# Causal attention with the value products of two units in a row, local attention with 64-row mask products

## What is computed

```
scores = q k^T / sqrt(8), masked where key > query
out    = softmax(scores) v, then a projection
```

```
x = attn_layer(shift_tokens(x)) + x      # 6 times
x = ffn_layer(shift_tokens(x)) + x
sim  = 8 * q k^T, masked outside a band of 32 keys before the query
out  = softmax(sim) v
```

## Time and profile before

| | us |
|---|---|
| Median of 3 runs | 5096.87 (5092.64 to 5099.63) |
| Profiled execution, device time | 5098.97 |
| Its span | 5097.2 |
| TensorE matmul busy | 4661.2 (91%) |
| VectorE busy | 3758.7 (74%) |
| ScalarE busy | 2797.7 (55%) |
| GpSimd busy | 2121.7 (42%) |

### The profile page before, as it was taken

The page is one execution under the profiler, slowest core; times in us unless marked ns, Lnnn a source line. Parts: engine busy times, 40 slices in busy tenths (PEclk is TensorE's granted clock), DMA queues, the critical chain, the costliest instruction groups (busy, mean ns, idle before and its releaser), DMA issues. The chain is left out here.

```text
span 5097.2 us, 170071 instructions
## 1 busy us (share of the span) xinstructions
PE 4661.2 (91%) x75792; PEld 2846.5 (56%) x75792; DVE 3758.7 (74%) x4270; ACT 2797.7 (55%) x3791; POOL 2121.7 (42%) x1691
## 2 busy tenths in 40 slices
PE   7858997999689869999999999999999999999998
PEld 5623333444233336774767567665776567747674
DVE  5667883333688659885898588867897688868895
ACT  4527774223477736554556556555565556546564
POOL 4330000001100046663666366635665466536661
PEclk9979998999799989999999999999999999999999
DMA  0021111000111121111111111111111111111110
GB/s 23 12 69 33 42 44 36 1 0 22 58 44 38 32 61 44 37 39 43 40 40 40 43 40 40 40 44 40 40 40 53 30 37 41 39 43 40 40 40 26
DMA packets 95786, 192.97 MB, mean 38 GB/s; under 512 B 27088, under 2 KB 45520, under 8 KB 93264
## 3 DMA queue, kind: packets, MB, share of 16 engines
q1 hardware_dynamic: 95056, 182.09, 14.0%
HBM read 60.36 MB, written 15.73 MB: 15 GB/s over the span
## 5 line engine op out<-in xcount | busy, mean ns | idle before, releaser
L1852 POOL TENSOR_TENSOR part_of_layer<-part_of_layer,sine_of_layer 128x512 f32<-128x512 f32 x768 | 963.1, 1276 | 628.4 <-DVE sine_of_layer L1728 628.4
L1863 POOL TENSOR_TENSOR part_of_layer<-part_of_layer,inverse_of_layer 128x1024 f32<-128x1024 f32 x384 | 730.2, 1902 | 262.0 <-ACT inverse_of_layer L1611 247.0
L969 ACT ACTIVATE prob_of_ca<-ps 128x1024 f32<-128x1024 f32 (+3 forms) x768 | 594.1, 814 | 261.5 <-PE ps L843 196.0
L1725 DVE TENSOR_TENSOR part_of_layer<-ps,rope 128x1024 f32<-128x1024 f32 x384 | 466.0, 1213 | 43.1 <-ACT square_of_layer L1599 41.4
L1728 DVE TENSOR_TENSOR sine_of_layer<-ps,rope 128x1024 f32<-128x1024 f32 x384 | 464.6, 1210 | 0.0
L861 PE MATMUL ps<-keys_of_ca,queries_of_ca 64*128 64x512 bf16 (+3 forms) x1536 | 330.5, 342 | 132.5 <-DVE top_of_ca L1001 60.8
L1642 ACT ACTIVATE values_of_layer<-ps 128x1024 f32<-128x1024 f32 x192 | 196.7, 1024 | 456.7 <-PE ps L1492 456.7
L1511 PEld LDWEIGHTS ps<-prob_t_of_layer,mixed_of_layer 64*64 64x64 f32 x12288 | 343.2, 134 | 167.2 <-issue 157.8
L1518 PE MATMUL ps<-heads_out_of_layer,wo 128*128 128x128 f32 x3072 | 415.7, 280 | 13.7 <-ACT heads_out_of_layer L1631 13.0
L1418 PE MATMUL ps<-qkv,shifted 128*128 128x512 f32 x768 | 387.0, 627 | 26.2 <-POOL values_of_layer L1866 20.3
L1764 DVE TENSOR_REDUCE total_of_layer<-prob_of_layer 128x16 f32<-128x1024 f32 x192 | 234.2, 1220 | 235.2 <-ACT prob_of_layer L1635 235.2
(11 more groups left out here) (206 smaller groups left out, 9203.6 us busy)
## 6 DMA issues: line engine op xcount, KB each, us to landing
mixed_of_layer<-values_of_layer SPq DMA_DIRECT2D x636, 128.0 KB
mixed_of_layer<-values_of_layer SPq DMA_DIRECT2D x264, 64.0 KB
queries_of_ca<-q_parts SPq DMA_DIRECT2D x384, 32.0 KB
keys_of_ca<-k_parts SPq DMA_DIRECT2D x384, 32.0 KB
qkv<-in_qkv SPq DMA_DIRECT2D x6, 1536.0 KB, 6.4
q_parts<-parts_of_ci SPq DMA_DIRECT2D x16, 384.0 KB, 2.6
k_parts<-parts_of_ci SPq DMA_DIRECT2D x16, 384.0 KB, 2.6
rope<-in_rope SPq DMA_DIRECT2D x6, 1024.0 KB, 9.0
```

What stands on the lines that cost most here:

```text
L969: nc.scalar.activation(prob[:, i % 2, 2 * two:2 * two + 2, j:], ps[:, 2 * two:2 * two + 2, j:], ACT.Exp, scale=scale).then_inc(raised, 1)
L1725: nc.vector.tensor_tensor(part[:, t % 2, side], by_head(slot), table(2 * side, t), ALU.mult).then_inc(parts, 1)
L1852: nc.gpsimd.tensor_tensor(out, out, sine[:, side, :, (1 - to) * half:(2 - to) * half], ALU.add).then_inc(rotated, 1)
L1863: nc.gpsimd.tensor_tensor(part[:, t % 2, side], part[:, t % 2, side], by, ALU.mult).then_inc(scaled, 1)
```

## The change

In causal attention, `prob` becomes a ring of three units. TensorE no longer does `weigh` once per unit; after the scores and maxima of every even unit it does it for the two units before, in a row. In local attention the mask products use 64 rows instead of 32: the stationary operand is a 64 by 32 piece of the identity, whose lower 32 rows are zero, and the moving operand 64 rows of the `band` table. The table repeats every 32 rows, so what is added is the same.

```
+PROBS = 3
-        prob = st.sb("prob", [P, 2, HG, CH])
+        prob = st.sb("prob", [P, PROBS, HG, CH])
...
-                                                prob[:, i % 2, h, j:], start=kt == 0, stop=kt == 4 * qc + 3)
+                                                prob[:, i % PROBS, h, j:], start=kt == 0, stop=kt == 4 * qc + 3)
...
-                    if u:
-                        weigh(*divmod(u - 1, NU))
-                weigh(ALL - 1, NU - 1)
+                    if u and u % 2 == 0:
+                        for done_unit in (u - 2, u - 1):
+                            weigh(*divmod(done_unit, NU))
+                for i in (NU - 2, NU - 1):
+                    weigh(ALL - 1, i)
...
-                            if u >= 2:
-                                act.wait_ge(weighed, u - 1)
-                            nc.scalar.activation(prob[:, i % 2, 2 * two:2 * two + 2, j:], ps[:, 2 * two:2 * two + 2, j:],
+                            if u >= PROBS:
+                                act.wait_ge(weighed, u - PROBS + 1)
+                            nc.scalar.activation(prob[:, i % PROBS, 2 * two:2 * two + 2, j:], ps[:, 2 * two:2 * two + 2, j:],
...
-                            rows = slice(h * WIN, (h + 1) * WIN)
-                            nc.tensor.matmul(two_banks(SCORE_SLOT)[i * WIN:(i + 1) * WIN, h, :], k["ident_b"][rows, rows],
+                            rows = slice(h * DH, (h + 1) * DH)
+                            nc.tensor.matmul(two_banks(SCORE_SLOT)[i * WIN:(i + 1) * WIN, h, :],
+                                             k["ident_b"][rows, h * DH:h * DH + WIN],
```

More of the change, by code:

```diff
@@ L687 @@
 AHEAD = NM - sum(map(sum, BETWEEN[:ROWS_UNIT]))
-assert sum(map(sum, BETWEEN)) == NM
+assert sum(map(sum, BETWEEN)) == NM and NU % PROBS == 0
 FINISH = {(0, 9): ("invert", 0), (1, 9): ("mix", 0), (2, 9): ("mix", 1)}
```

## The result

The kernel after takes 5212.90 us (median of 4 runs, 5203.38 to 5219.64), the kernel before 5096.89 beside it: ratio 1.0228, 95% interval 1.0212 to 1.0243, so 108 to 124 us slower. The profiled execution took 5212.54, its span 5210.8. In the new kernel most lines are one to four higher: L862 is the maxima product, L898 the score, L913 `weigh`, L1004 and L1006 the reductions of pairs with two and four pieces, L998 that of a lone product.

A forecast was written before the change was run, and what follows sets the result against it. TensorE's list was taken to bound local attention, and waits on the single pair buffer to decide causal attention. Profiled 5098.97 + 105 (causal) - 19 (masks) = 5185, or 5183 as a median; range 5125 to 5220.

The forecast's parts named there:

- part 1: Causal attention: fewer changes of the array's shape around value products save 1.55 us per group, 50 us in all.
- part 3: Local attention, 64-row masks: 0.24 instead of 0.34 us from masks to scores, 0.10 per tile, -19 us (0 to -25).
- Part 2: Causal attention: value products no longer cover VectorE's reductions between pair products; 4.8 us of new waits per group.
- The walk: One causal-attention group stepped through in the new order with the earlier durations: 31.84 us instead of 28.55, +105 us overall.
- its first two terms: Causal attention, shape changes: 0.10 us saved going into a value product and 0.09 going out of it.
- Its third term: Causal attention: a lone product no longer stands before a value product and can overlap its successor, gaining 0.07 us.
- Third buffer and copies: Causal attention: third buffer costs and frees nothing; sum copies at most 0.5 us later, counted nothing (32 us if uncovered).
- Have a group's time: Causal attention: SyncE's `collect` and GpSimd's copy of values follow `weighed` and have a group's time to spare.
- 0.27 can go before VectorE's own chain would bind: Local attention: of VectorE's 1.19 us wait per tile, 0.27 can go, so the tile follows TensorE's shorter list.
- A: Faster: causal attention's new waits do not come and TensorE's work is the limit; 5028 us, chance 0.08.
- B: About even: half of causal attention's new waits come, 2.4 us per group; 5105 us, chance 0.07.
- C: Waits as forecast, but no gain from equal shapes in causal or local attention; +154, 5251 us, chance 0.06.

The follow-up runs named there:

- ring alone: Kernel before with only the ring of three probabilities, value products in their old places: 5091.05 us, ratio 1.0005.
- the loop open: Kernel before, GpSimd's key scaling held until VectorE's `even` ends, except in a layer's last tile: 5072.91 us; with 64-row masks 5067.47.

## Why the prediction was right, and where it was off

**Direction and range held; the size was 30 us short** (+86 forecast, +116 measured). The measured sum: 32 x 2.96 = 95 for the waits less what part 1 saved, about 22 for the clock (216 instructions at 1.65 per 16), nothing for the masks. That 5213 stayed inside the range was partly luck: the top of 5220 made room for part 3 at nothing and for a delay of the copies. The first came; in place of the second, which did not, came the clock, for which the sum has no term.

**Part 2 was right.** One pair buffer and one value product as its cover decided it. The walk gave 31.84 for a group and the trace has 31.51; each pair of units is within 0.17. Product 0 is 1.80 behind product 25 (1.70 forecast; the masked product of 512 columns, 1.83, is the one to take there). The value products follow at 0.89 (0.91). VectorE is 71% busy in the stretch and idle during the double value products. The last group of each attention cost less than the others, not the same: 27.6 and 27.5 against 26.16. And the 174 us that the prediction gives as time in which TensorE stands still count weight loads and products together; the products alone have 60.8. The walk does not use that number.

**The step that failed in part 2 is one that it lacks:** the walk took every duration at the clock of before. The earlier trace rows showed 1.00 for a TensorE that was 90% busy. The change put waits of 1.11 and 1.08 us within 2 us of each other in front of the longest f32 products, and these ran at 1.2 GHz in every second group. The idle time that I added up as waits was charged a second time.

**Part 1** was about right. Two value products in a row take 1.86 to the next score (425.81 to 427.67), one alone took 1.00, and the step into them is taken once instead of twice: some 0.23 to 0.25 saved where its first two terms have 0.19. Its third term, 0.07 for the lone product, was not measured apart. As a whole, the idle time noted in a group rises from 2.92 to 6.96 us while the group grows by 2.96, so at least 1.08 per group came back of the 1.55 forecast. It is more than 1.08, since idle notes leave out part of each wait (1.11 noted for 1.27 in the earlier trace rows) and there are six more waits.

**Third buffer and copies:** nothing, as forecast; ring alone +1. "Have a group's time" was too broad: one unit more of delay for the copies, and 37.6 us of waits for a DMA stood there.

**Part 3: the size of the saving was right, its worth was not.** 0.34 to 0.226 against 0.24 forecast. The Trainium skill's rule on weight loads ("TensorE: Matmul & The Clock Gate", part 3), which would have made it nothing, does not hold here: 64-row masks share their rows with the scores, and the time fell all the same. In the tile shown the scores' first weight load starts at 2628.57, while masks that started at 2628.55 are under way on the same rows. The failed sentence is "0.27 can go before VectorE's own chain would bind". I looked for slack in VectorE's idle time in a tile and took the durations of its operations as fixed. `even` is not: it is stretched until GpSimd is done, and so looks like work while it is a wait. Tiles that repeat to 0.01 us should have said that a closed loop holds them; a loop of TensorE's list alone would have shortened by what the list lost. The loop explains the 13.81 that did not move. That the program gained nothing also has to do with the scores, which took back part of the saving with the loop open too.

**The rivals:** A and B are out, since the groups are 31.51 and more; C is out too: it meant groups of 28.55 + 4.8 = 33.35, and where the clock holds they are 31.51.

## What to carry over

Before moving work off a place on an in-order engine, ask which single buffer it covered, and walk the list once around the period with the turnaround of that buffer. Here the length of the period came out to 1% (31.84 against 31.51) and its growth to a tenth (3.29 against 2.96). Then look at what stands still in the new order: waits of about 1 us ahead of heavy products can cost TensorE its clock, and cheap products into a free bank can keep it. And where a period repeats exactly, follow the loop that closes on itself before you price a saving; an operation whose duration varies with its start is part of a wait.

## What the runs showed of the chip

TensorE's granted clock fell to half for about 3 us after two waits of 1.11 and 1.08 us in a program that otherwise kept it busy, and 8 throw-away products per group in these waits mostly prevented it. A VectorE multiplication of 128 x 1024 f32 with both inputs in SBUF took 1.22 us alone and up to 2.15 beside a GpSimd one. Holding GpSimd back until it was done gave the program 19 us.
